# Running sums of a linear-attention block: from triangular matrix products on TensorE to scans on VectorE, with a new reciprocal and new scaling of q and k

## The chip, the cores and the metric

The kernel runs on one core of one Trainium2 chip. The metric is the device time of the whole kernel in microseconds. Before the change it is 269.14 us, the median of three runs (268.63 to 271.65). A core has a matrix engine (TensorE, PE in the rows, with its weight load PEld), a vector engine (VectorE, DVE), a scalar engine for functions such as exp and ln (ScalarE, ACT), a general engine (GpSimd, POOL) and SyncE (SP), which issues transfers. Each works through its own list of instructions in order, and they wait for each other by semaphores.

## The reference, cut to what matters

```
h = layernorm(x) * (1 + ca) + sa                 # x: (8, 512, 128); ca, sa per batch entry
qkv = einsum('btd,ed->bte', rms_norm(h), w_qkv)
q, k, v = split(qkv, 3)
q = rms_norm(q);  k = rms_norm(k)
w  = exp(k)
kv = cumsum(w * v, axis=1);  w = cumsum(w, axis=1)      # running sums over the 512 tokens
y  = sigmoid(q) * kv / (w + 1e-06)
u, g = split(einsum('bte,fe->btf', y, w_swiglu), 2)
x  = x + ga * (h + einsum('btd,ed->bte', u * silu(g), w_out))
h2 = layernorm(x) * (1 + cb) + sb
x  = x + gb * moe(h2)      # top 1 of 16 experts with capacity 320, each gelu(h2 @ w1) @ w2
```

The attention has no score matrix: its core is two running sums over the tokens of each batch entry, one of exp(k) and one of exp(k)·v.

## The kernel before, in words

The kernel has two phases. The first makes attention and routing for the eight batch entries (512 tokens of 128 channels each, four tiles of 128 tokens). The second runs the experts, two at a time, on rows that were scattered to HBM, and scatters the results to the output. The change touches the first phase alone. The second starts when the last of the 32 row scatters of the first has landed.

The order of the first phase is written out by hand. Every engine calls `batches` with a list of pairs (lag, step); in round i it runs, in the order of its list, each step for batch entry i − lag. So in a round an engine works for up to six batch entries, from lag 0 (layer norm, projection of q and k) over lag 1 (RMS norms, exponentials), 2 (running sums), 3 (output projections with their gate), 4 (residual, second norm) to 5 (router, scatter). There are 13 rounds, 0 to 12. Since an engine does its list strictly in order, one step that waits holds all that stand behind it, in its round and the next.

TensorE's PSUM banks are shared in the same way. `claim(pe, bank, reader, b)` makes TensorE wait, before it writes a bank, until the previous content was read, and names the semaphore by which the new content will count as read. Bank "g" is used in turn by `project_g`, `h2_back` and `transpose_q`; bank "qk" by `project_qk` alone.

The steps that matter:

- `project_qk(i)` (L878) makes q and k of one entry in bank "qk", tokens on partitions. `square_sums` (L470, ScalarE) takes their squares, `qk_means` and `rms_scales` make one scale per token. `normalize_qk` (L651, VectorE) multiplies all eight 128x128 tiles with their scales in one instruction of 1024 columns, from PSUM into the buffer `qkn`; with that the bank is free. `exp_qk` (L486, ScalarE) takes the exponential of `qkn` in one instruction of 1024 columns. (The weights of q are negated, so that exp(−q) comes out.)
- `weigh_v` (L660, VectorE) multiplies v by exp(k). `pair_sums` (L383, GpSimd) adds tiles 0 and 1. `running_sum` (L901, TensorE) multiplies with a triangle of ones, five matmuls per sum, which gives the running sum with channels on partitions; it is called for w and for kv.
- `transpose_q` (L894) turns exp(−q). `log_q` and `log_w` (L494, L499, ScalarE) take ln(1 + exp(−q)) and ln(w + 1e-6), GpSimd adds them (`log_denominator`, L389), and `reciprocal` (L504) takes exp(−sum). `divide` (L670, VectorE) multiplies the running sum of kv, from PSUM, by it: `yT`.
- `project_g` (L920) and `project_u` (L925) multiply `yT` with the gate weights. `clamp_g` (L676, VectorE) copies g out; `exp_g`, `log_g`, `sigmoid_g` (ScalarE) and `silu` (L395, GpSimd) make the gate, `gate_u` (L682) the product, `project_out` (L930) the output projection.
- `top1`, `top_prob`, `slots` (L712 to L758, VectorE) route the tokens; `gate_rows` and `scatter` (L401, L410, GpSimd) write 512 rows to HBM with four indirect transfers per entry.

## Time and profile before

| | |
|---|---|
| median of three runs | 269.14 us (268.63 to 271.65) |
| span of the profiled execution | 268.4 us; no other time of that execution is listed |
| TensorE matmul busy | 204.6 us (76%), 1171 instructions |
| VectorE busy | 150.2 us (56%), 450 instructions |
| ScalarE busy | 147.3 us (55%), 387 instructions |
| GpSimd busy | 125.7 us (47%), 130 instructions |
| phase 1, to the end of the last scatter's issue | 154.04 us |
| phase 2 | 114.4 us |

The engines' busy times count instructions at work, not waits. Matmuls are pipelined, and their ends are modelled: of two matmuls in a row, the distance of their starts says more than their lengths. A row of the timeline merges neighbouring instructions of one line (x8 is eight of them), and gives their start, the time from the first start to the last end, and in brackets the idle time of the engine just before, with what ended it. The granted clock of TensorE is 1.00 at 2.4 GHz and 0.50 at 1.2 GHz.

### The profile page before, as it was taken

To read this page: it belongs to the slowest core of one execution; us is meant where nothing else is said; L and a number is where in the kernel's file an instruction comes from. 1 tells how busy PE (TensorE), PEld (TensorE's weight loads), DVE (VectorE), ACT (ScalarE), POOL (GpSimd) and SP (SyncE) were. 2 spreads that over 40 slices of the span, in tenths; PEclk is the share of its full clock that TensorE was granted. 3 is DMA by queue.
4 is the path that set the end of the run, shared out by engine and by line. 5 is a ranking of instruction groups with operands and counts; after the bars stand their busy time and mean duration, and the time that the engine had idled before them with its cause. 6 is when DMAs were issued, how large, how long until landed. Compare 5 with 4: busy or idle time off the path is not lost.

```text
span 268.4 us, 4054 instructions
## 1 busy us (share of the span) xinstructions
PE 204.6 (76%) x1171; PEld 170.2 (63%) x1171; DVE 150.2 (56%) x450; ACT 147.3 (55%) x387; POOL 125.7 (47%) x130
## 2 busy tenths in 40 slices
PE   1999999999998999888565017797787779689800
PEld 1886888888887888666454017586575658468500
DVE  4466757868989796866964221435625253454310
ACT  3274896888786886754644024573735447273100
POOL 4111324415492857584666610018446363745670
PEclk9999999999999999997886555999999999999975
DMA  5999991101040404030332159330649374760400
GB/s 184 312 361 359 334 324 52 42 1 39 4 158 0 161 0 161 0 140 29 131 117 87 42 131 298 82 129 17 194 156 297 94 263 112 244 197 26 129 31 0
DMA packets 32901, 36.51 MB, mean 136 GB/s; under 512 B 2431, under 2 KB 26950, under 8 KB 32880
## 3 DMA queue, kind: packets, MB, share of 16 engines
q1 hardware_dynamic: 29552, 29.20, 34.9%
q0 software_dynamic: 3328, 7.07, 7.4%
q8 instruction: 9, 0.15, 0.2%
q14 instruction: 12, 0.10, 0.1%
HBM read 19.19 MB, written 18.95 MB: 142 GB/s over the span
## 4 chain that ended last, share of the span: by engine, by line
PE 43%; DVE 17%; issue 12%; DMA 10%; ACT 7%; POOL 6%; SPq 2%; POOLq 1%; DVEq 0%; ACTq 0%
POOL out_dram L441 6%; DMA w<-in_L_ffn_w_dram 5%; PE bank L1054 5%; PE bank L882 5%; PE bank L923 3%; PE bank L952 3%; PE bank L1064 3%; DVE cand L722 3%; PE bank L935 2%; PE bank L906 2%; PE bank L904 2%; PE bank L907 2%; PE bank L937 2%; PE bank L874 2%; DMA out_dram<-x_all,rest 2%
## 5 line engine op out<-in xcount | busy, mean ns | idle before, releaser
L441 POOL DMA_INDIRECT out_dram<-x_all,rest x40 | 48.6, 1214 | 58.3 <-DVE x_all L837 48.2
L607 ACT ACTIVATE HT<-bank 128x320 f32<-128x320 f32 x64 | 27.7, 438 | 41.7 <-PE bank L1054 23.4
L1064 PE MATMUL bank<-HT,w 128*128 128x320 f32 x128 | 37.8, 438 | 12.2 <-DVE qkn L849 12.2
L417 POOL DMA_INDIRECT dispatched_rows<-rows,slot x32 | 31.7, 991 | 14.2 <-issue 7.9
L1064 PEld LDWEIGHTS bank<-HT,w 128*128 128x128 f32 x128 | 23.3, 190 | 21.7 <-DVE qkn L849 14.1
L819 DVE TENSOR_TENSOR w1l<-w,w1h 128x1024 fp32r<-128x1024 f32 x8 | 15.9, 1992 | 27.4 <-ACT w1h L582 25.3
L1054 PE MATMUL bank<-xth,w1h 128*128 128x320 f32 x64 | 23.3, 364 | 4.7 <-DMA w<-in_L_ffn_w_dram 3.1
L582 ACT CAST w1h<-w 128x1024 fp32r<-128x1024 f32 x8 | 16.3, 2034 | 8.5 <-DMA dispatched_rows<-rows,slot 8.5
L1054 PE MATMUL bank<-xth,w1l 128*128 128x320 f32 x64 | 20.4, 319 | 0.0
L1054 PE MATMUL bank<-xtl,w1h 128*128 128x320 f32 x64 | 20.4, 319 | 0.0
L399 POOL TENSOR_TENSOR gs<-gc,sg 128x512 f32<-128x512 f32 x8 | 10.2, 1275 | 19.2 <-ACT lw L502 14.0
L832 DVE TENSOR_TENSOR junk<-bank,rest 128x640 f32<-128x640 f32 (+2 forms) x9 | 6.8, 751 | 20.4 <-PE bank L1035 18.1
L882 PE MATMUL bank<-wqkvT,hT 128*128 128x256 f32 x64 | 17.7, 425 | 0.2
L1054 PEld LDWEIGHTS bank<-xth,w1h 128*128 128x128 f32 x64 | 12.7, 199 | 7.0 <-issue 4.6
L475 ACT ACTIVATE junk<-bank 128x128 f32<-128x128 f32 x64 | 16.6, 297 | 0.2 <-PE bank L882 0.2
L1028 PE MATMUL bank<-ident,hin 128*128 128x128 f32 x40 | 6.3, 292 | 13.1 <-DMA hin<-dispatched_rows 13.1
L533 ACT ACTIVATE xh<-rows,nm,rs 128x128 f32<-128x128 f32 x32 | 13.2, 481 | 5.1 <-DVE nm L709 5.0
L849 DVE COPY qkn<-bank 128x320 f32<-128x320 f32 x16 | 7.8, 488 | 14.3 <-PE bank L1064 8.9
L935 PE MATMUL bank<-diag_ga,hT 128*128 128x128 f32 x64 | 14.6, 315 | 1.0 <-DVE GT L686 1.0
L475 ACT ACTIVATION_READ_ACCUMULATOR junk<-bank 128x1 f32 x64 | 14.7, 230 | 0.0
L380 POOL TENSOR_TENSOR hsq<-hT 128x512 f32<-128x512 f32 x8 | 8.3, 1044 | 13.5 <-ACT hT L467 13.5
L1028 PEld LDWEIGHTS bank<-ident,hin 128*128 128x128 f32 x40 | 5.2, 150 | 14.6 <-DMA hin<-dispatched_rows 13.2
(156 smaller groups left out, 532.6 us busy)
## 6 DMA issues: line engine op xcount, KB each, us to landing
w<-in_L_ffn_w_dram SPq DMA_DIRECT2D x16, 512.0 KB, 5.6
dispatched_rows<-blank SPq DMA_DIRECT2D x8, 965.0 KB, 12.6
rest<-dispatched_rows SPq DMA_DIRECT2D x8, 645.0 KB
hin<-dispatched_rows SPq DMA_DIRECT2D x8, 320.0 KB, 4.3
x_all<-in_L_attn_x_dram SPq DMA_DIRECT2D x8, 256.0 KB, 5.1
out_dram<-rows SPq DMA_DIRECT2D x8, 256.0 KB
out_dram<-x_all,rest POOLq DMA_INDIRECT x40
dispatched_rows<-rows,slot POOLq DMA_INDIRECT x32
```

The source lines that it names most:

```text
L417: pool.indirect_dma_start(out=disp_d, out_offset=bass.IndirectOffsetOnAxis(ap=slot[:, b, j:j + 1], axis=0), in_=rows[:, b, j, :], in_offse ...
L441: pool.indirect_dma_start(out=out_d.rearrange("b t d -> (b t) d"), out_offset=bass.IndirectOffsetOnAxis(ap=rest[par][:, n, C_TOK - D:C_TOK ...
L475: last = act.activation(junk[:, 2 * j + m, :], ps_qk[:, j, m * D:(m + 1) * D], ACT.Square, accum_out=ssq[:, j, m:m + 1])
L533: last = act.activation(xh2[:, j, :], rows[:, b, j, C_X1:C_X1 + D], ACT.Identity, bias=nm2[:, j:j + 1], scale=rs2[:, j:j + 1])
L582: act.copy(w1h[par][:, :, :, :], w1[par][:, :, :].rearrange("p e (m f) -> p e f m", f=NF)).then_inc(w1h_done, 1)
L607: act.activation(HT[e][:, f, :], ps_h[c % HB][:, 0:CAP], ACT.Gelu_apprx_tanh).then_inc(h_done, 1)
L819: dve.tensor_tensor(w1l[par][:, :, :, :], w1[par][:, :, :].rearrange("p e (m f) -> p e f m", f=NF), w1h[par][:, :, :, :].bitcast(f32), ALU ...
L882: last = pe.matmul(ps_qk[:, j, :], hT[b % NHT][:, j * P:(j + 1) * P], wqkvT[:, 0:2 * D], start=True, stop=True)
L935: pe.matmul(ps_u[:, j * P:(j + 1) * P], hT[b % NHT][:, j * P:(j + 1) * P], diag_ga[:, b, :], start=True, stop=False)
L1028: last = pe.transpose(ps_xt[:, n * P:(n + 1) * P], hin[par][:, n, :], ident[:, :])
L1054: last = pe.matmul(ps_h[c % HB][:, 0:CAP], w[par][:, e, f, :], x[par][:, e * CAP:(e + 1) * CAP], start=(n == 0), stop=(n == 2))
L1064: last = pe.matmul(ps_o, w2[par][:, e, f, :], HT[e][:, f, :], start=(f == 0), stop=(f == NF - 1))
```

## The change

Running sums. The triangular matmuls and `pair_sums` go. TensorE transposes exp(k) and exp(k)·v as it does exp(−q) (`to_channels`, four transposes each), and VectorE runs two `tensor_tensor_scan` instructions over the 512 tokens of a channel, `scan_w` and `scan_kv`, from PSUM into SBUF. A new tile `ones`, filled by GpSimd at the start, is the factor of the scans.

Denominator. VectorE makes (1 + exp(−q))·w in one instruction (`denominator`); ScalarE takes one logarithm of it in place of two, and `reciprocal` stays.

Product. `divide` moves from VectorE to GpSimd, and reads the two factors from SBUF. On GpSimd it stands first in a round, where `silu` stood, behind the scatters of the round before.

Scaling of q and k. `normalize_qk` and `qkn` go. `exp_qk` is now eight instructions of 128 columns that read q or k from PSUM, with the token's scale as the instruction's scale. Bank "qk" is free when they have ended. Bank "g", when `transpose_q` has filled it, is free when `denominator` has read it, in place of `log_q`.

```diff
-        qkn = sb("qkn", [P, 2 * NJ, D])
-
-        ewkv = [sb(f"ewkv{n}", [P, NJ + 1, 3, D]) for n in range(2)]
-        lq = sb("lq", [P, T])
-        lw = sb("lw", [P, T])
+        ones = sb("ones", [P, T])
+
+        ewkv = [sb(f"ewkv{n}", [P, NJ, 3, D]) for n in range(2)]
+        wsum = sb("wsum", [P, T])
+        kvsum = [sb(f"kvsum{n}", [P, T]) for n in range(2)]
+        den = sb("den", [P, T])
...
+            pool.memset(ones[:, :], 1.0).then_inc(pool_setup, 1)
...
-            def pair_sums(b):
...
-            def log_denominator(b):
...
+            def divide(b):
+                after(pool, rden_done, b)
+                after(pool, kvsum_done, b)
+                after(pool, u_ps, b, 1)
+                pool.tensor_tensor(yT[:, :], kvsum[b % 2][:, :], rden[:, :], ALU.mult).then_inc(yT_done, 1)
...
             batches([
-                (3, silu), (2, log_denominator), (0, squares), (5, gate_rows),
-                (1, pair_sums), (5, scatter)])
+                (3, divide), (3, silu), (0, squares), (5, gate_rows), (5, scatter)])
...
             def exp_qk(b):
-                after(act, qkn_done, b)
-                after(act, sumkv_ps, b, 2)
+                after(act, nrr_done, b)
+                after(act, kvT_ps, b, 2)
                 after(act, eqT_ps, b, 2)
-                act.activation(ewkv[b % 2][:, 0:NJ, 0:2, :].rearrange("p j m d -> p j (m d)"),
-                               qkn[:, :, :].rearrange("p (j m) d -> p j (m d)", m=2),
-                               ACT.Exp).then_inc(ew_done, 1)
-
-            def log_q(b):
...
-            def log_w(b):
...
+                t = ewkv[b % 2]
+                for j in range(NJ):
+                    for m in range(2):
+                        last = act.activation(t[:, j, m, :], ps_qk[:, j, m * D:(m + 1) * D], ACT.Exp,
+                                              scale=nrr[:, 2 * j + m:2 * j + m + 1])
+                last.then_inc(ew_done, 1)
+
+            def log_denominator(b):
+                after(act, den_done, b)
+                after(act, rden_done, b, 1)
+                act.activation(lden[:, :], den[:, :], ACT.Ln).then_inc(lden_done, 1)
...
             batches([
-                (5, normalize2), (3, reciprocal), (0, ln1_scale), (2, log_q),
+                (5, normalize2), (3, reciprocal), (0, ln1_scale),
                 (1, square_sums), (5, modulate2), (3, exp_g), (1, rms_scales), (3, log_g),
-                (2, log_w), (3, sigmoid_g), (0, modulate1), (4, ln2_scale), (5, h2_rows),
+                (2, log_denominator), (3, sigmoid_g), (0, modulate1), (4, ln2_scale), (5, h2_rows),
                 (5, exp_logits), (1, exp_qk)], early=(ln1_scale,), second=copy_rows)
...
-            def normalize_qk(b):
-                after(dve, nrr_done, b)
...
-                dve.tensor_tensor(qkn[:, :, :], ps_qk.rearrange("p j (m d) -> p (j m) d", m=2),
-                                  nrr[:, 0:2 * NJ].unsqueeze(2).to_broadcast([P, 2 * NJ, D]), ALU.mult
-                                  ).then_inc(qkn_done, 1)
...
-            def divide(b):
...
+            def scan_w(b):
+
+                after(dve, ekT_ps, b)
+                after(dve, den_done, b, 1)
+                dve.tensor_tensor_scan(wsum[:, :], ones[:, :], ps_w, 1e-06, ALU.mult, ALU.add
+                                       ).then_inc(wsum_done, 1)
+
+            def scan_kv(b):
+                after(dve, kvT_ps, b)
+                after(dve, yT_done, b, 2)
+                dve.tensor_tensor_scan(kvsum[b % 2][:, :], ones[:, :], ps_kv, 0.0, ALU.mult, ALU.add
+                                       ).then_inc(kvsum_done, 1)
+
+            def denominator(b):
+                after(dve, eqT_ps, b)
+                dve.wait_ge(wsum_done, b + 1)
+                after(dve, lden_done, b, 1)
+                dve.scalar_tensor_tensor(den[:, :], ps_g, 1.0, wsum[:, :], ALU.add, ALU.mult
+                                         ).then_inc(den_done, 1)
...
             batches([
-                (0, stats1), (0, aggregate1), (2, weigh_v), (3, divide), (0, normalize1),
-                (1, h_means), (3, clamp_g), (4, residual), (1, qk_means), (4, stats2),
-                (1, normalize_qk), (4, aggregate2), (5, top1), (4, shift2), (3, gate_u),
+                (0, stats1), (0, aggregate1), (2, weigh_v), (0, normalize1), (2, scan_w),
+                (1, h_means), (2, denominator), (3, clamp_g), (4, residual), (1, qk_means), (4, stats2),
+                (2, scan_kv), (4, aggregate2), (5, top1), (4, shift2), (3, gate_u),
                 (5, top_prob), (5, slots)], early=(stats1, aggregate1, normalize1), second=diagonals)
...
             def project_qk(b):
                 after(pe, hT_done, b)
-                claim(pe, "qk", qkn_done, b)
+                claim(pe, "qk", ew_done, b)
...
+            def to_channels(ps, t, m):
+
+                for j in range(NJ):
+                    last = pe.transpose(ps[:, j * P:(j + 1) * P], t[:, j, m, :], ident[:, :])
+                return last
+
             def transpose_q(b):
                 after(pe, ew_done, b)
-                claim(pe, "g", lq_done, b)
...
-            def running_sum(ps, t, m):
...
-            def sum_w(b):
-                after(pe, pair_done, b)
-                claim(pe, "w", lw_done, b)
...
-            def sum_kv(b):
-                after(pe, pair_done, b)
-                claim(pe, "kv", yT_done, b)
...
+                claim(pe, "g", den_done, b)
+                to_channels(ps_g, ewkv[b % 2], 0).then_inc(eqT_ps, 1)
+
+            def transpose_k(b):
+                after(pe, ew_done, b)
+                claim(pe, "w", wsum_done, b)
+                to_channels(ps_w, ewkv[b % 2], 1).then_inc(ekT_ps, 1)
+
+            def transpose_kv(b):
+                after(pe, kv_done, b)
+                claim(pe, "kv", kvsum_done, b)
+                to_channels(ps_kv, ewkv[b % 2], 2).then_inc(kvT_ps, 1)
...
             batches([
-                (5, transpose2), (1, h_square_sums), (3, project_g), (2, sum_w),
-                (0, transpose1), (2, sum_kv), (5, logits), (5, h2_back), (3, project_u),
+                (2, transpose_k), (5, transpose2), (1, h_square_sums), (3, project_g),
+                (0, transpose1), (2, transpose_kv), (5, logits), (5, h2_back), (3, project_u),
                 (1, project_v), (5, ranks), (0, project_qk), (1, transpose_q),
                 (3, project_out)], early=(transpose1,), second=row_products)
```

Three places in the lists of instructions follow, before and after. Names to the left of the arrow are written, those to the right read; the brackets give the semaphores that an instruction waits for.

TensorE in round 4, from the sums of squares of entry 3 to the running sum of kv of entry 2. Before:

```order
L874 MATMUL bank<-tri,hsq 128x1 [waits kv_done,hsq_done]
L874 MATMUL bank<-tri,hsq 128x1 x3
L923 MATMUL bank<-yT,wswT 128x512 [waits lq_done,yT_done]
L904 MATMUL bank<-tri,ewkv 128x256 [waits lw_done,pair_done]
L905 MATMUL bank<-tri,ewkv 128x128
L906 MATMUL bank<-tri,ewkv 128x256
L907 MATMUL bank<-tri,ewkv 128x256
L908 MATMUL bank<-tri,ewkv 128x128
L867 MATMUL bank<-ident,xh 128x128 [waits hT_done,xh_done]
L867 MATMUL bank<-ident,xh 128x128 x3
L904 MATMUL bank<-tri,ewkv 128x256 [waits yT_done,pair_done]
```

The same place with the change:

```order
L895 MATMUL bank<-ident,ewkv 128x128 [waits wsum_done,ew_done]
L895 MATMUL bank<-ident,ewkv 128x128 x3
L872 MATMUL bank<-tri,hsq 128x1 [waits kv_done,hsq_done]
L872 MATMUL bank<-tri,hsq 128x1 x3
L916 MATMUL bank<-yT,wswT 128x512 [waits den_done,yT_done]
L865 MATMUL bank<-ident,xh 128x128 [waits hT_done,xh_done]
L865 MATMUL bank<-ident,xh 128x128 x3
L895 MATMUL bank<-ident,ewkv 128x128 [waits kvsum_done,kv_done]
L895 MATMUL bank<-ident,ewkv 128x128 x3
```

The transposes of exp(k) (`transpose_k`, first two rows) stand ahead of the sums of squares, the ten triangular matmuls are four transposes and four, and `project_g` (L923, now L916) waits for `den_done` in place of `lq_done`: its bank was filled by `transpose_q` of the next entry at the end of the round before.

TensorE later in round 4, around `project_qk` of entry 4. Before, and then with the change:

```order
L928 MATMUL bank<-yT,wswT 128x512 [waits x1_done,yT_done]
L890 MATMUL bank<-wqkvT,hT 128x128 [waits nrm_a,hT_done]
L890 MATMUL bank<-wqkvT,hT 128x128 x3
L882 MATMUL bank<-wqkvT,hT 128x256 [waits qkn_done,hT_done]
L882 MATMUL bank<-wqkvT,hT 128x256 x3
L898 MATMUL bank<-ident,ewkv 128x128 [waits gc_done,ew_done]
```

```order
L921 MATMUL bank<-yT,wswT 128x512 [waits x1_done,yT_done]
L888 MATMUL bank<-wqkvT,hT 128x128 [waits nrm_a,hT_done]
L888 MATMUL bank<-wqkvT,hT 128x128 x3
L880 MATMUL bank<-wqkvT,hT 128x256 [waits ew_done,hT_done]
L880 MATMUL bank<-wqkvT,hT 128x256 x3
L895 MATMUL bank<-ident,ewkv 128x128 [waits gc_done,ew_done]
```

The order is the same; `project_qk` (L882, now L880) waits for the exponentials of the entry before (`ew_done`), where it waited for their normalisation (`qkn_done`).

GpSimd from the end of round 5 into round 7. Before:

```order
L399 TENSOR_TENSOR gs<-gc,sg 128x512 [waits GT_done,sg_done,gc_done]
L393 TENSOR_TENSOR lden<-lq,lw 128x512 [waits rden_done,lw_done,lq_done]
L380 TENSOR_TENSOR hsq<-hT 128x512 [waits mh_ps,hT_done]
L405 TENSOR_TENSOR rows<-gb_row,prob 128x4x128 [waits prob_done]
L386 TENSOR_TENSOR ewkv<-ewkv 128x256 [waits kv_done]
L417 DMA dispatched_rows<-rows,slot 5120x386 [waits slot_done,h2_done,gp_done]
L417 DMA dispatched_rows<-rows,slot 5120x386 x3
```

With the change:

```order
L389 TENSOR_TENSOR yT<-kvsum,rden 128x512 [waits u_ps,kvsum_done,rden_done]
L395 TENSOR_TENSOR gs<-gc,sg 128x512 [waits GT_done,sg_done,gc_done]
L382 TENSOR_TENSOR hsq<-hT 128x512 [waits mh_ps,hT_done]
L401 TENSOR_TENSOR rows<-gb_row,prob 128x4x128 [waits prob_done]
L413 DMA dispatched_rows<-rows,slot 5120x386 [waits slot_done,h2_done,gp_done]
L413 DMA dispatched_rows<-rows,slot 5120x386 x3
```

`yT` is now made here, as the first thing of a round, and so directly behind the four scatters (L413) of the round before. The additions of tiles (L386) and of logarithms (L393) are gone.

## Rows read from the trace of the kernel before

**Rows 1.** The page: busy tenths of TensorE in 40 slices of the span.

```profile
PE   1999999999998999888565017797787779689800
```

**Rows 2.** Windows cut at the ends of `clamp_g` in rounds 3, 4 and 10 (columns as named).

```profile
core 0: us, PE busy (x) PEld busy (x) DVE busy (x) ACT busy (x) POOL busy (x), PEclk, DMA share, GB/s
36.26:47.63 11.37, 11.37 (x74) 9.85 (x73) 6.83 (x24) 8.19 (x30) 4.23 (x4) 1.00 0.45 168
47.63:127.82 80.19, 74.23 (x492) 63.53 (x490) 63.19 (x224) 59.55 (x176) 45.96 (x45) 0.98 0.18 61
127.82:268.40 140.58, 88.79 (x473) 71.82 (x472) 58.16 (x114) 59.20 (x104) 66.62 (x58) 0.87 0.42 133
```

**Rows 3.** Groups by line: busy us, mean ns of one, idle before.

```profile
L656 DVE TENSOR_TENSOR qkn<-bank,nrr 128x1024 f32<-128x1024 f32 x8 | 9.7, 1214 | 1.8 <-ACT nrr L484 1.8
L393 POOL TENSOR_TENSOR lden<-lq,lw 128x512 f32<-128x512 f32 x8 | 10.2, 1276 | 5.9 <-ACT lw L502 5.9
L475 ACT ACTIVATE junk<-bank 128x128 f32<-128x128 f32 x64 | 16.6, 297 | 0.2 <-PE bank L882 0.2
L533 ACT ACTIVATE xh<-rows,nm,rs 128x128 f32<-128x128 f32 x32 | 13.2, 481 | 5.1 <-DVE nm L709 5.0
```

**Rows 4.** Timeline, ScalarE in round 4: from `exp_g` to `exp_qk` (start us, length us).

```profile
47.67 0.63 ACT L512 ACTIVATE eg<-gc 128x512 f32<-128x512 f32 x1 [1.51 <-DVE gc L680]
51.50 1.04 ACT L490 ACTIVATE ewkv<-qkn 128x1024 f32<-128x1024 f32 x1
```

**Rows 5.** Timeline, TensorE: parts of rounds 4 and 5.

```profile
46.74 0.59 PE L904 MATMUL bank<-tri,ewkv 128*128 128x256 f32 x2
...
48.48 0.60 PE L867 MATMUL bank<-ident,xh 128*128 128x128 f32 x4
...
52.41 1.89 PE L882 MATMUL bank<-wqkvT,hT 128*128 128x256 f32 x8
54.14 0.60 PE L898 MATMUL bank<-ident,ewkv 128*128 128x128 f32 x4
54.58 0.39 PE L935 MATMUL bank<-diag_ga,hT 128*128 128x128 f32 x2
...
56.37 0.60 PE L945 MATMUL bank<-ident,xh 128*128 128x128 f32 x4
...
57.61 1.10 PE L923 MATMUL bank<-yT,wswT 128*128 128x512 f32 x2
```

**Rows 6.** Timeline, round 9: `project_g` on TensorE and `clamp_g` on VectorE.

```profile
113.12 1.12 PE L923 MATMUL bank<-yT,wswT 128*128 128x512 f32 x2 [1.20 <-DVE yT L674]
...
114.28 0.69 DVE L680 TENSOR_SCALAR gc<-bank 128x512 f32<-128x512 f32 x1 [1.22 <-PE bank L923]
```

**Rows 7.** Timeline, round 10: `clamp_g` and the end of `slots` on VectorE.

```profile
127.13 0.69 DVE L680 TENSOR_SCALAR gc<-bank 128x512 f32<-128x512 f32 x1 [2.32 <-PE bank L923]
...
134.50 0.17 DVE L757 SCALAR_TENSOR_TENSOR slot<-sl_a,sl_o 128x4 int32<-128x4 f32 x1
```

**Rows 8.** Timeline, GpSimd: first scatter of entry 5, and what follows its fourth.

```profile
135.55 1.01 POOL L417 DMA_INDIRECT dispatched_rows<-rows,slot  x1 [1.52 <-DVE slot L757]
...
140.41 1.07 POOL L405 TENSOR_TENSOR rows<-gb_row,prob 128x512 f32<-128x512 f32 x1
```

**Rows 9.** Windows around a gap of TensorE in round 9 (columns of Rows 2).

```profile
119.87:122.10 2.23, 0.29 (x6) 0.20 (x5) 2.16 (x6) 0.60 (x3) 0.92 (x1) 0.99 0.00 0
122.25:125.30 3.05, 3.05 (x14) 3.05 (x15) 2.49 (x9) 1.42 (x4) 1.28 (x2) 0.50 0.00 0
```

**Rows 10.** Timeline, start of the kernel and rounds 1 and 2.

```profile
7.00 0.90 PE L992 MATMUL bank<-ident,wqkv 128*128 128x128 f32 x3 [0.59 <-DMA gw<-in_L_ffn_gate_w_dram]
...
17.52 0.76 ACT L467 ACTIVATE hT<-bank,mod 128x512 f32<-128x512 f32 x1
...
19.02 2.28 PE L882 MATMUL bank<-wqkvT,hT 128*128 128x256 f32 x8
...
26.46 1.11 DVE L632 TENSOR_SCALAR xh<-x_all,mv,rs 128x128 f32<-128x128 f32 x4 [2.64 <-ACT rs L460]
```

49 lines of the change are left out of this document (9 added, 40 removed).

## The prediction, as put on record before the result was known

> **What bounds the kernel now.** The page's slices come first: TensorE is at nine tenths or more in nearly all of the first fifteen slices, so the first half of phase 1 is TensorE's [rows 1]. Then windows, cut at the ends of `clamp_g` in rounds 3, 4 and 10, which I use as marks C3, C4 and C10. Round 4 takes 11.4 us, and TensorE is busy in all of it. The six rounds from C4 to C10 take 80.2 us, 13.4 each, with VectorE and TensorE both well loaded. From C10 on, 140.6 us are tail and experts, which the change leaves as they are: no scan, no exponential of q and k and no product for the gate is left after C10 [rows 2]. So the forecast is one question: when does C10 come? Since each engine follows its list, I look for chains that close over one round, and price them.
>
> **Prices.** A scan over 512 columns: no row shows one. A pass of 512 columns with a PSUM operand takes 0.69 [rows 6], one of 1024 columns 1.21 [rows 3]. I take 1.21, because each column needs the sum before it, and keep 0.69 for the range. The Trainium skill ("DVE: opcode table, instruction layouts, handler registers and perf-mode slots", Datapath and trigger behaviour) says that the built-in scan runs at half throughput; no row of before shows that, and by it the sum would stay as it is. `denominator`: 512 columns, 0.69. The product on GpSimd: an addition of the same shape there takes 1.28 [rows 3].
>
> An exponential of 128 columns with a per-token scale: `square_sums` has the shape and PSUM source, 0.30 each [rows 3], and eight with their accumulator reads fill about 2 us, 0.25 each; `normalize2` has a per-token scale, 0.48 each [rows 3], about 0.39 from start to start as they overlap. I take the middle, 0.32, so 2.6 for eight against 1.05 for the one instruction of before; the ends are 2.0 and 3.1. The Trainium skill ("ScalarE: Activation LUTs", Rules for kernel authors) budgets 0.3 us per activation and 0.83 ns per element. By it eight would be some 3.3 us, an estimate from that page, and the forecast 2 to 3 us later.
>
> **What goes.** Per round TensorE loses two running sums of 1.74 (46.74 to 48.48) and gains eight transposes, of which four take 0.44 (54.14 to 54.58) [rows 5]: 2.6 less. GpSimd loses `pair_sums` and swaps an addition for a product of the same price. VectorE loses `normalize_qk` (1.21) and `divide` (0.69) and gains 3.1. The new memset delays GpSimd's constants by about half a microsecond at most; TensorE waits until 7.00 for the weights of the gate anyway, 0.59 of it idle in front of the first transposes [rows 10]. It costs nothing, and 0.5 if that load came earlier.
>
> **What the new waits close.** Two chains.
>
> Chain A, from C to the next C, for rounds that make a `project_qk`: ScalarE works from `exp_g` to the start of the exponentials, 3.8 (47.67 to 51.50; one logarithm stands where one stood) [rows 4]; the exponentials 2.6; only then is bank "qk" free, so `project_qk` 1.73, `transpose_q` 0.44, `project_out` 1.79 (52.41, 54.14, 54.58, 56.37), then `transpose_k` 0.60 [rows 5]; `scan_w` 1.21; `denominator` 0.69; only now is bank "g" free for `project_g`: 1.16 to the start of `clamp_g` and 0.69 for it (113.12, 114.28) [rows 6]. Sum 14.8. The transposes and square sums that TensorE does beside `scan_w` take 1.24 [rows 5], so they end with it. In the late rounds `h2_rows` and `exp_logits` add some 0.6: 15.4.
>
> Chain B, for rounds behind a scatter (C5 to C10, five periods): from C to the end of `slots`. In round 10 this is 127.82 to 134.67, 6.9 [rows 7]; with `scan_kv` (1.21) and `qk_means` in it 8.2. Then the scatters: 134.67 to 140.41, 5.7 [rows 7, 8]. GpSimd now has `divide` behind them, 1.28; `project_g` and `clamp_g` 1.85. Sum 17.1. Before, `divide` was on VectorE and did not see the scatters.
>
> The clock. In round 9 TensorE had next to nothing to do for 2.2 us (119.87 to 122.10), then worked at 1.2 GHz: the granted clock was 0.50 over the next 3 us of full work [rows 9]. With chain A TensorE has nothing from the end of `project_v` to the end of the exponentials, over 4 us in each round from 2 on. I expect `project_qk` to be done at half clock each time: 1.7 more. In the late rounds chain A is then 17.1, level with B.
>
> **The sum.** Round 1: `modulate1` starts at 17.52, the exponentials behind it end at 20.8, so `project_qk(1)` starts at 20.9 where it started at 19.02, 1.9 later [rows 10]. The row products behind it and their copies on ScalarE shift as much, and so does `normalize1` of round 2, which waits for ScalarE: 26.46 becomes 28.4, its end 29.5 [rows 10]. Then `scan_w` 30.7, `denominator` 31.4, on ScalarE the RMS scales, the logarithm and `modulate1`, 1.8 (an estimate: the 3.8 of [rows 4] without the three passes of the gate and the scale of the second norm), 33.2, exponentials 35.8; from there to C3 as in chain A, 6.5 without the parts on ScalarE before and with `transpose_q` and without `project_out`: 42.3. Before it was 36.26: +6.0.
>
> Two periods of A bring C5 to 71.9. Half clock for `project_qk` in rounds 2, 3 and 4 adds 5.1: 77.0. Five periods of 17.1 bring C10 to 162.5, where it was 127.82: +34.7. The rest stays 140.6. Span 303.1. The median of the runs is 0.7 above the profiled span, so 303.8; **I say 304**, 13% slower.
>
> **The rivals.**
>
> 1. The clock holds: no `project_qk` falls to half. For it: in rounds 2 to 8 it held at 1.00 or just below through waits of 1 to 2 us [rows 2]. Against it: [rows 9], and the new gaps are twice as long. Then A is 14.8 and 15.4, B still 17.1, C10 at 157.4: 299. With the short prices, scans of 0.69 (0.5 less in four early rounds and five late ones) and exponentials of 2.0 (0.6 in four), 7 less again: 292. Chance 0.22.
>
> 2. The clock stays at half for longer than `project_qk`, over `transpose_q`, `project_out` and `transpose_k` too: 2 to 2.5 more in each of the six rounds with a projection, which also lifts A above B in the late ones: 312 to 318. Chance 0.10.
>
> 3. Faster: TensorE's relief decides, in rounds 2 to 4, where it has no idle time [rows 1, 2]. Three times 2.6 is 7.8: 261. It needs both new holds on a bank to be over when TensorE arrives: the exponentials would have to end within the `project_u` and `project_v` before, 2 us after C. But ScalarE alone needs 3.8 from C to their start. The point is there, and the rows put it out of reach by 4 us. Chance 0.04.
>
> 4. No change: the early rounds gain these 7.8 and the scatters in front of `divide` cost as much late, 268 to 271. It needs the same as rival 3. Chance 0.02.
>
> The forecast itself, both chains with half clock for the projection and prices near mine, has 0.62. Its own spread: 0.5 on a scan in nine periods, 0.5 on the exponentials in four to seven, and the length of `top1` and `slots`, which GpSimd's work stretches or not, 0.5 in five.
>
> **Range and chances.** From the low prices on a clock that holds partly (288) to the longer half clock (319). What this kernel's measurement can tell from no change is about 1%. Faster by more: 0.04, rival 3. Within 1%: 0.03, rival 4 and a little besides. Slower: 0.93.
>
> **What would show it.** In the trace after: the wait of `project_qk` for the exponentials is among TensorE's longest; `project_g` waits for VectorE's `denominator` in rounds 3 to 5 and for GpSimd's product in rounds 6 to 10; in these the product starts where the fourth scatter ends. C3 near 43 to 44, C5 near 77, C10 near 162, and from C10 to the end 140. The granted clock is 0.50 in a stretch of each round from 2 to 7. TensorE's busy time per round is lower at full clock, and VectorE's scans last 1.2. I am wrong if the product finds GpSimd free before the scatters, if the exponentials overlap to 0.2 each, or if C10 to the end has changed by more than a microsecond or two, as that part should not know of the change.

## The result, and the profile after

| | before | after |
|---|---|---|
| median (lowest to highest) | 269.48 us (268.63 to 271.65), 4 runs | 307.90 us (304.58 to 311.29), 4 runs |
| ratio | | 1.139, 95% interval 1.133 to 1.145 |
| span of the profiled execution | 268.4 us | 302.8 us, the fastest of the four (its time 304.58) |
| TensorE matmul busy | 204.6 us | 200.1 us, 1075 instructions |
| VectorE, ScalarE, GpSimd busy | 150.2, 147.3, 125.7 us | 159.2, 150.7, 121.3 us |

The change makes the kernel 14% slower. No engine's busy time rose by more than 9 us, yet 34.4 us were added to the span: the engines wait for each other. The medians take all runs, the ratios leave out single runs in a slower state (one each of the changed kernel, e3 and e5, and one of the kernel before, 531 us, beside e8 and e9).

The page after, TensorE's busy tenths and granted clock in 40 slices; against [rows 1]:

```profile
PE   2978586758576966855737660187795796887910
PEclk9999979979989778897885955569999999999985
```

The nines of the first half are gone. Windows after, cut as in [rows 2] at the ends of `clamp_g` in rounds 3, 4 and 10 (us, busy us of PE, PEld, DVE, ACT, POOL with counts, granted clock, DMA share, GB/s):

```profile
43.99:58.17 14.18, 9.77 (x65) 8.20 (x63) 7.97 (x26) 8.52 (x34) 3.54 (x3) 0.98 0.00 0
58.17:163.79 105.62, 70.28 (x413) 57.36 (x411) 68.66 (x229) 61.77 (x206) 44.33 (x41) 0.86 0.15 52
163.79:302.80 139.01, 89.55 (x473) 71.77 (x473) 59.08 (x114) 59.19 (x104) 64.53 (x56) 0.86 0.41 130
```

(43.99 is C3, 58.17 is C4.) Round 4 takes 14.2 us in place of 11.4, with TensorE busy for 9.8 of them; the six rounds up to C10 take 105.6 in place of 80.2. What follows C10 is as long as it was, 139.0 against 140.6. Marks C3 to C10 after: 43.99, 58.17, 74.65, 92.38, 111.79, 129.22, 146.69, 163.79.

Groups by line after (busy us, mean ns of one, idle before and what ended it):

```profile
L880 PE MATMUL bank<-wqkvT,hT 128*128 128x256 f32 x64 | 24.0, 541 | 14.7 <-ACT ewkv L488 14.7
L488 ACT ACTIVATE ewkv<-bank,nrr 128x128 f32<-128x128 f32 x64 | 17.3, 385 | 0.0
L916 PE MATMUL bank<-yT,wswT 128*128 128x512 f32 x16 | 12.5, 872 | 19.4 <-POOL yT L389 10.1 <-DVE den L671 9.3
L389 POOL TENSOR_TENSOR yT<-kvsum,rden 128x512 f32<-128x512 f32 x8 | 10.3, 1282 | 5.4 <-ACT rden L500 5.3
L658 DVE TENSOR_TENSOR_SCAN wsum<-ones,bank 128x512 f32<-128x512 f32 x8 | 9.8, 1220 | 15.7 <-PE bank L895 12.4 <-remote 3.3
L671 DVE SCALAR_TENSOR_TENSOR den<-bank,wsum 128x512 f32<-128x512 f32 x8 | 5.5, 687 | 0.1
L505 ACT ACTIVATE eg<-gc 128x512 f32<-128x512 f32 x8 | 5.0, 630 | 34.7 <-DVE gc L678 34.7
```

The chains can be read from these waits: `project_qk` (L880) waits for the exponentials (L488), 14.7 us; `scan_w` (L658) for the transposes behind it; `project_g` (L916) for `denominator` (L671) and for GpSimd's product, 19.4 together; and ScalarE, before the gate's exponential (L505), for `clamp_g`. Before, 0.2 us went to `project_qk`'s wait.

Round 4 on TensorE after; [rows 5] has it before (start, length, in brackets the idle time before and what ended it):

```profile
49.53 1.97 PE L880 MATMUL bank<-wqkvT,hT 128*128 128x256 f32 x8 [3.00 <-ACT ewkv L488]
51.33 0.60 PE L895 MATMUL bank<-ident,ewkv 128*128 128x128 f32 x4
...
53.55 0.60 PE L895 MATMUL bank<-ident,ewkv 128*128 128x128 f32 x4
53.99 0.95 PE L872 MATMUL bank<-tri,hsq 128*128 128x1 f32 x8
56.35 1.10 PE L916 MATMUL bank<-yT,wswT 128*128 128x512 f32 x2 [1.41 <-DVE den L671]
```

Round 10 after, GpSimd; against [rows 7, 8]:

```profile
154.79 1.01 POOL L413 DMA_INDIRECT dispatched_rows<-rows,slot  x1 [1.52 <-DVE slot L755]
156.11 0.97 POOL L413 DMA_INDIRECT dispatched_rows<-rows,slot  x1 [0.30 <-issue]
157.39 0.97 POOL L413 DMA_INDIRECT dispatched_rows<-rows,slot  x1 [0.30 <-issue]
158.66 0.98 POOL L413 DMA_INDIRECT dispatched_rows<-rows,slot  x1 [0.30 <-issue]
159.64 1.30 POOL L389 TENSOR_TENSOR yT<-kvsum,rden 128x512 f32<-128x512 f32 x1
```

and TensorE, which had worked at full clock until 154.4, in the same round:

```profile
160.99 2.07 PE L916 MATMUL bank<-yT,wswT 128*128 128x512 f32 x2 [6.58 <-POOL yT L389]
```

The product starts where the fourth scatter ends, TensorE waits 6.6 us for it, and `project_g` then takes 2.07 in place of 1.10: half clock (the granted clock of 147.00 to 154.40 is 1.00, that of 160.99 to 163.06 is 0.50).

### The profile page after: what moved, and what is told of

It is laid out like the page before. It is cut to its first block and busy times, and to the rows that moved or that the text cites. A ratio compares the mean times of both kernels' runs of the same rounds, so it can differ in the third digit from the quotient of the medians.

```text
span 302.8 us, 3902 instructions
## 1 busy us (share of the span) xinstructions
PE 200.1 (66%) x1075; PEld 161.7 (53%) x1075; DVE 159.2 (53%) x458; ACT 150.7 (50%) x435; POOL 121.3 (40%) x123
## 5 line engine op out<-in xcount | busy, mean ns | idle before, releaser
L413 POOL DMA_INDIRECT dispatched_rows<-rows,slot x32 | 31.6, 988 | 18.7 <-DVE slot L755 9.7
L1057 PEld LDWEIGHTS bank<-HT,w 128*128 128x128 f32 x128 | 23.3, 190 | 21.8 <-DVE ewkv L847 14.2
L880 PE MATMUL bank<-wqkvT,hT 128*128 128x256 f32 x64 | 24.0, 541 | 14.7 <-ACT ewkv L488 14.7
L395 POOL TENSOR_TENSOR gs<-gc,sg 128x512 f32<-128x512 f32 x8 | 10.1, 1266 | 57.1 <-issue 48.2
L880 PEld LDWEIGHTS bank<-wqkvT,hT 128*128 128x128 f32 x64 | 16.4, 268 | 18.7 <-issue 15.6
L916 PE MATMUL bank<-yT,wswT 128*128 128x512 f32 x16 | 12.5, 872 | 19.4 <-POOL yT L389 10.1
L505 ACT ACTIVATE eg<-gc 128x512 f32<-128x512 f32 x8 | 5.0, 630 | 34.7 <-DVE gc L678 34.7
L382 POOL TENSOR_TENSOR hsq<-hT 128x512 f32<-128x512 f32 x8 | 9.2, 1153 | 26.7 <-ACT hT L462 26.7
L658 DVE TENSOR_TENSOR_SCAN wsum<-ones,bank 128x512 f32<-128x512 f32 x8 | 9.8, 1220 | 15.7 <-PE bank L895 12.4
L895 PE MATMUL bank<-ident,ewkv 128*128 128x128 f32 x96 | 17.3, 314 | 1.1 <-ACT ewkv L488 1.1
L678 DVE TENSOR_SCALAR gc<-bank 128x512 f32<-128x512 f32 x8 | 5.5, 692 | 22.8 <-PE bank L916 22.8
L488 ACT ACTIVATE ewkv<-bank,nrr 128x128 f32<-128x128 f32 x64 | 17.3, 385 | 0.0
L895 PEld LDWEIGHTS bank<-ident,ewkv 128*128 128x128 f32 x96 | 14.4, 168 | 4.8 <-issue 2.8
```

Of the source, the lines that this page charges most:

```text
L413: pool.indirect_dma_start(out=disp_d, out_offset=bass.IndirectOffsetOnAxis(ap=slot[:, b, j:j + 1], axis=0), in_=rows[:, b, j, :], in_offse ...
L488: last = act.activation(t[:, j, m, :], ps_qk[:, j, m * D:(m + 1) * D], ACT.Exp, scale=nrr[:, 2 * j + m:2 * j + m + 1])
L880: last = pe.matmul(ps_qk[:, j, :], hT[b % NHT][:, j * P:(j + 1) * P], wqkvT[:, 0:2 * D], start=True, stop=True)
L895: last = pe.transpose(ps[:, j * P:(j + 1) * P], t[:, j, m, :], ident[:, :])
L916: pe.matmul(ps_g, wswT[:, D:2 * D], yT[:, :], start=True, stop=True).then_inc(g_ps, 1)
L1057: last = pe.matmul(ps_o, w2[par][:, e, f, :], HT[e][:, f, :], start=(f == 0), stop=(f == NF - 1))
```

## The experiments

The table has the marks and the verdicts; the texts on record and what follows from each stand below. "Loss" is the span over that of the kernel before, 268.4. Each ratio is to the kernel before as it ran beside that group (medians 269.5 beside e1, e3 and e4, 269.75 beside e2b, e5, e6 and e7, 269.7 beside e8 and e9, 269.5 for the change). One difference in these spans is no effect of an edit that a run here shows: the first `project_qk` starts at 11.8 to 12.1 in e1, e3, e2b and e7 and at 10.7 to 11.1 in the others, and what follows shifts with it. So a difference of 1 us between two spans says little.

| | what it is | median us | ratio to before (95%) | span | loss | C3 | C5 | C10 |
|---|---|---|---|---|---|---|---|---|
| before | | 269.7 | | 268.4 | | 36.3 | 59.5 | 127.8 |
| after | the change | 307.9 | 1.139 (1.133 to 1.145) | 302.8 | 34.4 | 44.0 | 74.7 | 163.8 |
| e1 | product on VectorE | 293.9 | 1.093 (1.084 to 1.102) | 291.5 | 23.1 | 45.2 | 75.9 | 152.8 |
| e3 | scatter behind the product | 295.1 | 1.095 (1.085 to 1.104) | 293.1 | 24.7 | 45.1 | 75.7 | 152.7 |
| e4 | TensorE kept busy | 301.5 | 1.119 (1.111 to 1.127) | 299.6 | 31.2 | 42.0 | 71.0 | 160.5 |
| e2b | normalisation on VectorE | 297.5 | 1.102 (1.096 to 1.107) | 296.5 | 28.1 | 40.6 | 66.3 | 155.9 |
| e5 | e1 and e2b | 283.8 | 1.048 (1.040 to 1.056) | 281.3 | 12.9 | 41.2 | 67.3 | 141.4 |
| e6 | before, with the exponentials alone | 275.3 | 1.019 (1.014 to 1.024) | 274.4 | 6.0 | 40.7 | 66.2 | 135.2 |
| e7 | before, with the scans alone | 277.6 | 1.031 (1.026 to 1.037) | 274.6 | 6.2 | 38.7 | 61.1 | 134.6 |
| e8 | e1, bank g freed earlier | 289.1 | 1.070 (1.060 to 1.079) | 287.7 | 19.3 | 43.6 | 75.2 | 145.0 |
| e9 | e5, bank g freed earlier | 277.4 | 1.030 (1.020 to 1.040) | 275.9 | 7.5 | 38.5 | 62.5 | 132.8 |

**e1: the product back on VectorE.** GpSimd's list, then VectorE's.

```diff
-                (3, divide), (3, silu), (0, squares), (5, gate_rows), (5, scatter)])
+                (3, silu), (0, squares), (5, gate_rows), (5, scatter)])
...
-                (0, stats1), (0, aggregate1), (2, weigh_v), (0, normalize1), (2, scan_w),
+                (0, stats1), (0, aggregate1), (2, weigh_v), (3, divide), (0, normalize1), (2, scan_w),
```

> The changed kernel with one part undone: the product of kv's running sum and the reciprocal stands on VectorE again, at its old place behind weigh_v, and so does not stand behind the scatters on GpSimd. My theory (two chains): in rounds 6 to 8 the chain over the two banks (A, 17 to 19 us with half clock) is as long as the chain over the scatters (B), so these rounds stay as they are, and only rounds 9 and 10, which have no projection of q and k, get shorter, to some 13 and 10.5 us from 17.5 and 17.1: 10 to 12 us less in all, C10 (the end of clamp_g in round 10) at 152 to 154 where it is 163.8. Rival 1 (the scatters in front of the product are the whole late loss): all five late periods go back to 13 to 15 us, 17 to 20 us less. Rival 2 (the scatters cost nothing, the banks are everything): within 2 us of the changed kernel.

As on record, C10 comes at 152.8. Rounds 5 to 8 take 14.80, 17.11, 17.09, 17.08, and rounds 9 and 10 14.73 and 10.96, where the changed kernel needs 17.47 and 17.10: 8.9 of the 11.0 us by which C10 is earlier. (Most of the others are round 7, which in the changed kernel is 2 us longer than its neighbours.) So chain B was what set rounds 9 and 10, and rounds 6 to 8 are chain A's as well. TensorE in round 6 of e1:

```profile
82.59 3.65 PE L880 MATMUL bank<-wqkvT,hT 128*128 128x256 f32 x8 [1.11 <-ACT ewkv L482]
91.13 1.10 PE L916 MATMUL bank<-yT,wswT 128*128 128x512 f32 x2 [1.01 <-DVE den L671]
```

`project_qk` takes 3.65 at half clock (1.97 at full), and `project_g` waits for `denominator`.

**e3: the product stays on GpSimd, the scatter moves behind it**, and so into the next round (lag 6 in place of 5).

```diff
-                (3, divide), (3, silu), (0, squares), (5, gate_rows), (5, scatter)])
+                (3, divide), (6, scatter), (3, silu), (0, squares), (5, gate_rows)])
```

> The changed kernel with the scatters moved one lag back, in the list of GpSimd behind the product: divide(i-3), then scatter(i-6), then silu(i-3). Nothing else. Chain B is gone without touching VectorE. My theory: like e1, 10 to 12 us less (C10 at 152 to 154), the late periods with a projection unchanged, the last two shorter; the end of the phase no later, since the last scatters are paced by slots. Rival 1: 17 to 20 us less. Rival 2 (GpSimd's silu, now behind the scatters, takes the place of the product): gate_u waits for silu and less than 5 us is gained.

It gains what e1 gains, with C10 at 152.7 against 152.8. What cost was the place of the product behind four scatters, not that GpSimd takes 1.28 for it where VectorE takes 0.69.

**e4: TensorE kept busy in the gap.** Matmuls without a reader stand behind `project_v`, three for each of the first four entries, two for the others.

```diff
+            def keep_busy(b):
+                if b > 0:
+                    pe.wait_ge(kvsum_done, b)
+                for j in range(3 if b < 4 else 2):
+                    pe.matmul(ps_kv, ident[:, :], tri[:, :], start=True, stop=True)
...
-                (1, project_v), (5, ranks), (0, project_qk), (1, transpose_q),
+                (1, project_v), (1, keep_busy), (5, ranks), (0, project_qk), (1, transpose_q),
```

> The changed kernel with two or three idle matmuls (512 columns, 0.94 us each, into bank kv after its scan has read it, results unused) behind project_v in every round, so that TensorE is not idle until the exponentials end. My theory (the half clock after the gap costs 1.2 to 2 us a round): project_qk takes 1.7 to 2 us instead of 2.8 to 3.6 in rounds 5 to 7, granted clock near 1.00 until C8, 4 to 6 us less against the profiled run of the changed kernel and up to 9 less in the medians, whose spread (304.6 to 308.6) goes with the clock. Rival (TensorE's clock is a bystander, chain B sets the late rounds anyway): within 2 us.

`project_qk` takes 1.97 for each entry from 1 on, and rounds 4 and 5 are 14.18 and 14.80 (14.18 and 16.48 in the changed kernel), what chain A gives at full clock. Rounds 6 to 10 take 17.98, 17.94, 17.95, 18.55 and 17.10, because chain B is now last. TensorE in rounds 6 and 7:

```profile
86.46 1.76 PE L916 MATMUL bank<-yT,wswT 128*128 128x512 f32 x2 [2.90 <-POOL yT L389]
...
104.08 2.07 PE L916 MATMUL bank<-yT,wswT 128*128 128x512 f32 x2 [2.54 <-POOL yT L389]
```

The wait moved from `project_qk` to `project_g`, and the half clock with it. What chain A gained late was given back by B, and 3.2 us of span and 6.4 of medians remained, less than the 4 to 6 and up to 9 on record, but more than the 2 of the rival.

**e2b: the normalisation on VectorE, one exponential of 1024 columns.** VectorE writes q and k, scaled, into `ewkv`, and the exponential works there in place; bank qk is free when VectorE has read it.

```diff
-                claim(pe, "qk", ew_done, b)
+                claim(pe, "qk", qkn_done, b)
...
-                (2, scan_kv), (4, aggregate2), (5, top1), (4, shift2), (3, gate_u),
+                (1, normalize_qk), (2, scan_kv), (4, aggregate2), (5, top1), (4, shift2), (3, gate_u),
...
+                act.activation(t, t, ACT.Exp).then_inc(ew_done, 1)
```

> The changed kernel, with VectorE again multiplying q and k by their scales from bank qk (1024 columns, 1.21 us) and one exponential of 1024 columns (1.05 us); bank qk is free when VectorE has read it. My theory, in which project_qk behind the exponentials closes the long chain of a round: TensorE no longer waits for exponentials, project_qk stays at full clock, C3 comes near 37 and C5 near 61 to 62 (74.65 in the changed kernel). In the late rounds VectorE's 1.21 us more come ahead of slots, so the chain through the scatters and the product is 18.3 instead of 17.1, and C10 comes at 152 to 154 (163.8), span 291 to 292, 11 to 13 us less than the changed kernel. Rival theory, the hold of bank g by denominator is the burden and that of bank qk costs little: the early periods stay at 14 to 16, and less than 4 us are gained.

The early part gains 8.3 us by C5, where the theory had 13: C5 is at 66.3, not 61 to 62, and C3 at 40.6, not 37. In part that is so since the first `project_qk` started 0.7 later in this run (11.76 against 11.04) and VectorE comes to `denominator` of round 3 only at 37.4, behind `normalize_qk`, `scan_kv` and `weigh_v`. The late rounds are 18.3, 18.5, 17.5, 17.8 and 17.5, chain B with 1.2 more on it in the first two; the whole gained 6.3 us of span and 10.4 of medians, less than the 11 to 13 on record. C10 is 7.9 earlier; 1.6 of that is lost after C10, in a part that the edit leaves as it is. What chain A gives up late, chain B takes.

A first form of this run, e2, with nearly the same expectation, kept the scaled q and k in a buffer of their own. It did not fit into SBUF (`rows` needs 49,408 bytes of a partition, 49,216 were left), which is why e2b works in place.

**e5: both undone**, with the edits of e1 and e2b together:

```diff
+                (0, stats1), (0, aggregate1), (2, weigh_v), (3, divide), (0, normalize1), (2, scan_w),
...
+                (1, normalize_qk), (2, scan_kv), (4, aggregate2), (5, top1), (4, shift2), (3, gate_u),
```

> Both of the parts undone that the theory blames: the normalisation and one exponential as in the run on bank qk, and the product back on VectorE behind weigh_v. Left of the change are scans and transposes in place of triangular matmuls, and one logarithm in place of two. Theory, the two undone parts explain nearly all: C3 near 37, early periods about 12.3 (chain over bank g through scan_w and denominator, or VectorE's own work), late rounds 16, 13 and 10.5, bound by VectorE, C10 at 131 to 133, span 270 to 274, against 304 to 309 for the changed kernel and 268.4 for the one before. Rival theory, the scans and the new hold on bank g by denominator are themselves a burden of 2 us and more in each round: span above 280.

Here I was wrong by 7 to 11 us: 281.3, with C3 at 41.2 and C10 at 141.4, as the rival had it (above 280). Neither exponentials nor scatters are left in the way, and still each round waits. VectorE in round 5:

```profile
63.32 1.22 DVE L663 TENSOR_TENSOR_SCAN wsum<-ones,bank 128x512 f32<-128x512 f32 x1
...
64.63 0.69 DVE L676 SCALAR_TENSOR_TENSOR den<-bank,wsum 128x512 f32<-128x512 f32 x1
66.60 0.69 DVE L683 TENSOR_SCALAR gc<-bank 128x512 f32<-128x512 f32 x1 [1.28 <-PE bank L921]
```

`denominator` must end before `project_g` may write bank g, and VectorE then has nothing until `project_g` ends. That is 0.69 of work and 1.28 of idle time in a round, 2.2 to 2.4 in rounds 3, 6 and 10, on an engine that is well loaded itself. Before, VectorE was idle at this place for 0.4 to 0.7 in rounds 3 to 8.

**e6: before, with eight scaled exponentials from bank qk, no `normalize_qk`.**

```diff
-                act.activation(ewkv[b % 2][:, 0:NJ, 0:2, :].rearrange("p j m d -> p j (m d)"),
...
+                        last = act.activation(t[:, j, m, :], ps_qk[:, j, m * D:(m + 1) * D], ACT.Exp,
+                                              scale=nrr[:, 2 * j + m:2 * j + m + 1])
...
-                claim(pe, "qk", qkn_done, b)
+                claim(pe, "qk", ew_done, b)
```

> The kernel before with one part of the change alone: eight exponentials of 128 columns from bank qk with the token's scale, no normalize_qk; bank qk is free when they have ended. Theory, the hold on bank qk costs much only together with the rest of the chain over bank g (scan_w and denominator behind transpose_q): here project_qk waits about 1 us in a round, no project_qk falls to half clock, the early periods become about 12.5 (11.4 before), the late rounds gain from VectorE's relief of 1.2 us what they lose, and the whole is 273 to 276, 4 to 6 us slower than before. Rival theory, this part alone carries most of the loss in rounds 2 to 7: 285 or more, with project_qk at half clock.

The span is as on record: 274.4. C3 is 4.4 later, most of the loss; rounds 4 and 5 take 12.26 and 13.27 (11.37 and 11.82), the five late ones 69.1 together (68.4), which fits that VectorE's relief of 1.2 a round pays for the hold there. Against the text, one `project_qk` did fall to half clock, that of entry 1: 3.01, behind a wait of 3.05. In round 4 of e6 the wait is short and the clock stays up:

```profile
46.25 1.97 PE L876 MATMUL bank<-wqkvT,hT 128*128 128x256 f32 x8 [0.65 <-ACT ewkv L493]
```

**e7: before, with transposes and scans in place of the matmuls, two logarithms, `normalize_qk` and the product where they were.** The factor of the scans is a column of ones read with stride 0; there is one buffer for `kvsum`.

```diff
+                dve.tensor_tensor_scan(wsum[:, :], tri[:, P:P + 1].to_broadcast([P, T]), ps_w, 0.0,
+                                       ALU.mult, ALU.add).then_inc(wsum_done, 1)
...
+                dve.tensor_tensor_scan(kvsum[:, :], tri[:, P:P + 1].to_broadcast([P, T]), ps_kv, 0.0,
+                                       ALU.mult, ALU.add).then_inc(kvsum_done, 1)
```

> The kernel before with one part of the change alone: transposes and two scans in place of the triangular matmuls and pair_sums; two logarithms, normalize_qk and the product stay where they were. Per round TensorE has 2.6 us less and VectorE 2.4 us more. Theory: rounds 2 to 4, which TensorE bounds, get shorter by up to half a microsecond each (11.4 to about 10.9, then VectorE bounds them), rounds 5 to 10 get longer by about as much as VectorE's share in their chain, 1 us where top1 and slots stand behind scan_kv, and the whole is 266 to 272, within 1.5% of the kernel before. Rival theory, the price of a scan on VectorE goes onto the path in full in every round, 2.4 us in eight rounds: 285 and more.

The span is 274.6 and the median 277.6, 2.6 and 5.6 above the upper end of what I expected; the rival's 285 is excluded. So both were off, mine by less. C3 is 2.4 later, 0.9 of it from the later start. Round 4 takes 10.61, 0.8 less than before, and round 5 11.83, as before: TensorE's relief exists, in one round. But rounds 6 and 7 take 16.0 each (14.5 and 15.2), and TensorE waits for `top1` 2.8 us in round 6 and 3.5 in 7 and 8. In round 8:

```profile
99.83 0.23 PE L974 MATMUL bank<-seen,ones_b 128*128 128x64 bf16 x1 [3.49 <-DVE oh L736]
...
100.05 3.76 PE L891 MATMUL bank<-wqkvT,hT 128*128 128x256 f32 x8
```

Round 8 takes 17.2 (13.95), and the whole `project_qk` is at half clock. Before, TensorE waited 0.4 to 1.2 us at this place in rounds 6 to 8. So the scans cost by 2.4 us a round more on VectorE, which TensorE waits for in the late rounds, and by what these longer waits do to TensorE's clock. How much is each was not separated.

**e8 and e9: bank g freed earlier.** `transpose_q` goes to the next round, behind `transpose_kv`, and `denominator` behind `clamp_g`. e8 is e1 with this, e9 is e5 with it.

```diff
-                (1, h_means), (2, denominator), (3, clamp_g), (4, residual), (1, qk_means), (4, stats2),
+                (1, h_means), (3, clamp_g), (4, residual), (2, denominator), (1, qk_means), (4, stats2),
...
-                (0, transpose1), (2, transpose_kv), (5, logits), (5, h2_back), (3, project_u),
-                (1, project_v), (5, ranks), (0, project_qk), (1, transpose_q),
+                (0, transpose1), (2, transpose_kv), (2, transpose_q), (5, logits), (5, h2_back), (3, project_u),
+                (1, project_v), (5, ranks), (0, project_qk),
```

> The kernel of the first run (the change with its product back on VectorE), with transpose_q moved on TensorE from behind project_qk into the next round, behind transpose_kv, and denominator on VectorE moved behind clamp_g and residual. So bank g goes from clamp_g to transpose_q, and project_g no longer waits for scan_w and denominator. Theory, chain A closes over that hold: without transpose_q, scan_w and denominator the chain is 12.4 by its own terms (3.8, 2.2 for the exponentials as measured, 1.73, 1.79, 0.60, about 0.8 for the sums of squares, 1.85) and 14.1 with project_qk at half clock, late 14.7 instead of 17.1; C10 comes at 142 to 144 (152.8 in the first run), span 281 to 284 (291.5). Rival theory, the hold of bank qk by the exponentials alone closes the chain and that of bank g is beside it: under 2 us gained.

> The kernel that has both the normalisation on VectorE and the product on VectorE (span 281.3), with the same move of transpose_q and denominator. There project_g waits for denominator in each round; VectorE is idle 1.28 to 1.8 us behind denominator. Theory, that hold is what this kernel loses against the one with two logarithms (274.6): early periods 11.3 to 12, late ones 15.1, 15.1, 13.4, 13.4 and 11, bound by VectorE, C3 near 39, C10 at 130 to 133, span 269 to 273, so as fast as the kernel before or up to 1.5% slower. Rival theory, the 0.69 us of denominator on VectorE is itself the price: span 279 or more.

e9 gained 5.4 us of span and 6.4 of medians, and its C10 (132.8) is 8.6 before that of e5 and 1.9 before that of e7 (0.8 of that is the start). So the move won back all that e5 had lost over e7 up to there, 6.7. C3 came at 38.5 as expected, C10 at the upper end, and the span at 275.9, 3 us above. These 3 us lie in the second phase, which the edit leaves as it is: from C10 to the end of the last row scatter e9 takes 27.5 (26.5 to 28.0 in the others but e8), and then TensorE waits once for the weights of an expert for 3.5 us, where it waits 1.8 at most in the other runs:

```profile
205.97 0.41 PE L1052 MATMUL bank<-xth,w1h 128*128 128x320 f32 x1 [3.50 <-DMA w<-in_L_ffn_w_dram]
```

VectorE in round 6 of e9 has idle times of 0.4 and 0.2 where e5 has 2.2 (1.3 in most rounds):

```profile
77.55 0.69 DVE L683 TENSOR_SCALAR gc<-bank 128x512 f32<-128x512 f32 x1 [0.38 <-PE bank L921]
...
79.05 0.69 DVE L676 SCALAR_TENSOR_TENSOR den<-bank,wsum 128x512 f32<-128x512 f32 x1 [0.22 <-PE bank L900]
```

e8 gained 3.8 us of span (4.8 of medians), not 8 to 10. Rounds 6 and 9 are 14.75 and 12.05 (17.11 and 14.73 in e1), but in rounds 4, 5, 7 and 8 `project_qk` falls to half clock, in 4 and 5 behind a longer gap than in e1 (3.6 and 3.4):

```profile
50.15 3.58 PE L880 MATMUL bank<-wqkvT,hT 128*128 128x256 f32 x8 [4.06 <-ACT ewkv L482]
65.52 3.75 PE L880 MATMUL bank<-wqkvT,hT 128*128 128x256 f32 x8 [4.29 <-ACT ewkv L482]
```

and their periods are 14.94, 16.71, 16.42 and 16.40. The half clock was in the theory, though; what it had too small is the chain at full clock, 14.75 in round 6 for 13.0. From C to the start of the exponentials it had 3.8, and 0.6 more late; in rounds 6 and 7 these are 5.3 (4.4 in e1), since `denominator` now stands in front of `qk_means`, and ScalarE waits for that:

```profile
91.57 0.21 ACT L470 ACTIVATE nrl<-nrm 128x12 f32<-128x12 f32 x1 [0.94 <-DVE nrm L634]
```

The way through bank qk is still closed behind the exponentials, so the rival was half right. From C10 to the end e8 takes 142.7, 2 to 4 us more than the others but e9. Of that, 2.3 lie before the end of the last scatter, mostly in round 11, where the matmuls of `logits` take 1.89 at half clock (1.07 in e1).

No version beat the kernel before. The nearest are e6 (1.9% slower), e9 and e7 (3.0% and 3.1%). All three are slower beyond the noise; for e6 the interval does not settle whether by more or less than 2%, and for e9 hardly.

**Where the 34.4 us are.** One way from before to after, one step at a time, in spans: transposes and scans +6.2 (e7), one logarithm behind `denominator` +6.7 (e5), exponentials from bank qk +10.2 (e1), product on GpSimd +11.3 (after). In medians, which take in all runs, the steps are +7.9, +6.2, +10.1 and +14.0, 38.2 together; the last is larger there because the profiled run of the changed kernel was its fastest. The parts are not additive: the exponentials cost 6.0 alone (e6; 5.6 in medians) and 10.2 on top of the hold of bank g (10.1). If the product on GpSimd stands beside them (after against e2b) it is 6.3 by the spans but 10.4 by the medians, so that figure is open. No run has eight exponentials with a bank that is free early, so what they cost by the hold of bank qk and what by taking 1.1 us longer on ScalarE is not separated. e5 and e7 also differ in a second buffer for `kvsum` and in where the normalised q and k lie, which I did not separate.

## Why the prediction was right

Predicted 304, in a range of 288 to 319; measured 307.9, and the profiled span that the sum aimed at was 302.8 for 303.1. Point by point:

- **"The forecast is one question: when does C10 come."** C10 was set at 162.5 and came at 163.8; the rest at 140.6 came at 139.0. Held. That the sum is off by 0.3 only is luck: C5 came 2.4 early, the five late periods took 3.6 more, the rest 1.6 less, and the profiled run was the fastest of four (the other three have spans of 305.4 to 309.5). All of it lies well inside the range; in all kernels above but e8 and e9 the rest is 138.7 to 140.6.
- **Scan 1.21.** Measured 1.22 and 1.21, against 0.69 for a pass of `denominator` with as many columns. The Trainium skill ("DVE: opcode table, instruction layouts, handler registers and perf-mode slots", Datapath and trigger behaviour) has the scan at half throughput; the trace agrees, with 1.8 times the pass of `denominator`, and as long as `normalize_qk` takes for 1024 columns.
- **Exponentials 2.6 for eight.** Mis-sized: 2.16 from the first start to the last end. Single rows have a mean of 385 ns, but they overlap. The middle between two rows was the wrong choice; `square_sums`, which reads PSUM as they do, was the right neighbour. The 3.3, an estimate from the Trainium skill ("ScalarE: Activation LUTs", Rules for kernel authors), is not what a row of eight takes here.
- **TensorE's relief, and the sign.** As on record: the matmul busy time fell by 4.5 us in all, since part of the work now runs at half clock, and it bought nothing. Rival 3 stayed out of reach. The new memset takes 0.53 us and moved the first `project_qk` by 0.1.
- **Round 1, C3.** `project_qk(1)` was set at 20.9 and started at 20.59; C3 was set at 42.3, or 44 with half clock, and came at 43.99. The half clock came in `project_qk(1)` (3.63) and in `project_g` of round 3 (2.04), not in `project_qk(2)`.
- **Chain A, 14.8 at full clock.** (Its terms add up to 14.7.) Round 4 ran at full clock and took 14.18. Of the difference, 0.4 is the exponentials. It closed as told: TensorE waits for the exponentials 3.0, `scan_w` for the transposes, `project_g` for `denominator`.
- **Half clock for `project_qk` in each round from 2 on.** Half right. It took 1.97 for entries 2 and 3, behind waits of 3.4 and 3.0, and 2.8 to 3.6 for entries 4 to 7. C5 was set at 77.0 and came at 74.65. With TensorE kept busy in e4, `project_qk` takes 1.97 throughout, so it is the gap that costs the clock. The gap, set at over 4 us, was 3.0 to 3.4 in rounds 2 to 4, and later it is in two pieces, 1.3 to 2.2 for `ranks` and 1.1 for the exponentials. What rival 1 had for it, a clock that held before "through waits of 1 to 2 us", was one wait of 1.19 in rounds 2 to 8; all others were under 0.5.
- **Chain B, 17.1 for five periods.** They took 17.73, 19.41, 17.43, 17.47 and 17.10. The 17.10 of round 10 is luck in part: the way to the end of `slots` took 7.2 where 8.2 was set, and `project_g` and `clamp_g` 2.85 for 1.85, since half clock was not in this chain's sum. Also, the text had `project_g` wait for the product in rounds 6 to 10: it waits for `denominator` in rounds 3 to 8, and for the product in 9 and 10 alone. The two chains are level in 6 to 8, as the text had it. e1 and e3 show it: take B away, and rounds 6 to 8 stay at 17.1 while 9 and 10 fall to 14.7 and 11.0.
- **Not foreseen: round 7, 19.41.** Two things were added. `project_g` ran at half clock (1.91). And `scan_w` started at 107.00, though by the rows its transposes ended at 105.4 and VectorE was free from 103.7; ScalarE started its next step, also behind transposes, at 107.06, 1.2 late. e1, e3 and e4 have no such round. It is open what held both; by the rows the granted clock was 1.00 there:

```profile
104.80 0.60 PE L895 MATMUL bank<-ident,ewkv 128*128 128x128 f32 x4
105.23 0.60 PE L938 MATMUL bank<-ident,xh 128*128 128x128 f32 x4
...
107.00 1.22 DVE L658 TENSOR_TENSOR_SCAN wsum<-ones,bank 128x512 f32<-128x512 f32 x1 [3.33 <-remote]
107.06 0.78 ACT L535 ACTIVATE h2T<-bank,mod 128x512 f32<-128x512 f32 x1 [2.10 <-PE bank L938]
```

The other three runs of the changed kernel had granted clocks of 0.83 to 0.87 (0.878 here), which would fit more rounds at half clock, but they left no rows.

- **The median** was put 0.7 above the profiled span, as before. It is 5.1 above: the changed kernel varies more from run to run (2% between the lowest and the highest), and the profiled execution was its fastest.

## What to carry to other kernels

When work is moved off the busiest engine, write down first which buffer each moved step now holds, until when, and what it stands in line behind: here 2.6 us less work per round on TensorE went with rounds that are 2.8 to 5.6 us longer, through bank qk, bank g and four scatters. Price the chain that closes over a round and not the step, since the exponentials that cost 6 us alone cost 10 where another hold closed the same round. A gap of TensorE could cost here its own length and then 1 to 1.7 us more in what comes next, and closing it in one place moves both to the next wait, as e4 shows.
